# Cross-attention and expert layer: the queries split in two, the transposes one place sooner, the key split one place later

## What is computed

```
x = x + attention(layernorm(x), ctx)          # softmax(q k^T / 4) v, then @ Wp + bp
x = x + ffn(layernorm(x))                     # x <- the line above
# ffn: rms norm, logits = xn @ router^T + bias, probs = softmax(logits)
#      idx = top 512 rows per expert, y = gelu(xe @ fc1 + b1) @ fc2 + b2
#      the gated y are added into their rows and divided by the sum of the row's gates
```

## Time and profile before

| | |
|---|---|
| median of 3 runs | 991.97 us (991.0 to 992.49) |
| the profiled execution | 991.08 us, of which 989.3 us is the span of the instructions |
| TensorE busy over the span | 856.6 us (87%), weight loads 731.7 us (74%) |
| VectorE | 748.6 us (76%) |
| ScalarE | 507.9 us (51%) |
| GpSimd | 596.5 us (60%) |
| attention_phase | to about 475 us |

### The profile page before, as it was taken

One profiled execution on the slowest core, in us unless ns is written; L12 is line 12 of the kernel. 1 busy time (PEld: TensorE's weight loads), 2 busy tenths in 40 slices (PEclk: granted clock), 3 DMA queues, 4 the chain that ended last, 5 costly groups with the idle time before them and its releaser, 6 DMA issues. The chain is left out here.

```text
span 989.3 us, 20836 instructions
## 1 busy us (share of the span) xinstructions
PE 856.6 (87%) x6067; PEld 731.7 (74%) x6067; DVE 748.6 (76%) x1660; ACT 507.9 (51%) x921; POOL 596.5 (60%) x564
## 2 busy tenths in 40 slices
PE   3889999999999999999631138999999999999995
PEld 3677878878888878877521026989999999999985
DVE  4578888888888888887378975898777778777642
ACT  1355566555665566655246305555555555555531
POOL 3246676666766676656532265588887666775345
PEclk9799999999999999999855558999999999999998
DMA  4355666655665566654232024366766665665333
GB/s 146 101 196 200 199 207 220 215 200 188 221 220 203 200 201 218 222 191 152 80 109 85 4 65 136 115 169 171 208 169 161 157 159 154 159 163 158 94 70 43
DMA packets 129540, 156.51 MB, mean 158 GB/s; under 512 B 22464, under 2 KB 104656, under 8 KB 129376
## 3 DMA queue, kind: packets, MB, share of 16 engines
q1 hardware_dynamic: 104096, 113.06, 35.0%
q0 software_dynamic: 15616, 25.70, 12.3%
q10 hardware_dynamic: 9792, 17.31, 4.7%
HBM read 74.93 MB, written 26.28 MB: 102 GB/s over the span
## 5 line engine op out<-in xcount | busy, mean ns | idle before, releaser
L574 DVE TENSOR_REDUCE NM<-bank 128x4 f32<-128x480 f32 x256 | 155.7, 650 | 67.2 <-PE bank L724 66.4
L411 ACT ACTIVATE PT<-bank 120x512 f32<-120x512 f32 x256 | 144.3, 603 | 37.8 <-PE bank L749 35.4
L348 POOL TENSOR_SCALAR XN<-X,mv,rstd 128x256 f32<-128x256 f32 x126 | 153.1, 1225 | 14.4 <-POOL rstd L343 13.5
L1631 PE MATMUL bank<-W2H,HH 128*128 128x256 f32 x512 | 145.5, 284 | 2.0 <-issue 2.0
L1633 PE MATMUL bank<-W2H,HL 128*128 128x256 f32 x512 | 144.3, 282 | 0.0
L1632 PE MATMUL bank<-W2L,HH 128*128 128x256 f32 x512 | 144.2, 282 | 0.0
L1092 POOL DMA_INDIRECT out_dram<-C,IO x60 | 111.6, 1859 | 52.2 <-issue 31.0
L1360 DVE TENSOR_TENSOR HL<-hf,HH 128x512 fp32r<-128x512 f32 x128 | 87.3, 691 | 50.1 <-ACT HH L1515 49.4
L532 DVE RECIPROCAL RR<-RC 128x256 f32<-128x256 f32 x64 | 111.5, 1743 | 7.3 <-DMA RC<-PVS 7.3
L749 PE MATMUL bank<-QX,KX 128*120 128x256 f32 x512 | 110.0, 308 | 5.0 <-DMA QX<-NMT 4.6
L724 PE MATMUL bank<-KX,QX 128*128 128x240 f32 x512 | 105.4, 308 | 10.1 <-DMA QX<-QH 3.4
(11 more groups left out here) (189 smaller groups left out, 1894.1 us busy)
## 6 DMA issues: line engine op xcount, KB each, us to landing
QX<-QH ACTq DMA_DIRECT2D x64, 256.0 KB
W<-w1T_dram SPq DMA_DIRECT2D x16, 1024.0 KB, 5.4
W<-w2T_dram SPq DMA_DIRECT2D x16, 1024.0 KB, 5.9
X<-x_dram SPq DMA_DIRECT2D x32, 256.0 KB, 3.0
QX<-QL SPq DMA_DIRECT2D x32, 256.0 KB
XB<-x_dram SPq DMA_DIRECT2D x32, 256.0 KB, 2.9
RC<-PVS SPq DMA_DIRECT2D x64, 128.0 KB, 2.1
OC<-PVS SPq DMA_DIRECT2D x64, 128.0 KB, 3.0
```

Of the source, the lines that this page charges most:

```text
L348: ins = pool.tensor_scalar(dst[:, t, :], src[:, t, :], mv[:, t, 0:1], rstd[:, t:t + 1], ALU.subtract, ALU.mult)
L411: act.activation(PT[u][0:M, HE * k:HE * (k + 1), :], score_bank(b, k // 2)[k % 2][0:M, :], ACT.Exp, scale=SCALE) \
L574: dve.tensor_reduce(NM[u][:, t, :].rearrange("p (f n e) -> p n e f", n=HN, e=HE)[:, n, :, :], smax_bank[q % 2][:, 0:4 * M].rearrange("p (e ...
L1631: pe.matmul(o, wh, xh, start=first, stop=False)
```

## The change

Calls are put in another order on TensorE and VectorE; nothing is added or taken away, and ScalarE's, GpSimd's and SyncE's programs are the same. On VectorE `low_keys` goes behind the second row maximum. On TensorE the queries' product is made in two calls (its waits stand in the first, its signal q_done in the second), `queries(0)` before `max_scores(6)` and `queries(1)` before `max_scores(7)`; `rows2` goes before `scores(4)`, `rows` before `max_scores(2)` and `scores(5)`; and `scores(5)` goes behind `max_scores(2)`, `scores(6)` behind `max_scores(3)`, so that scores 6 and 7 stand side by side.

```diff
@@ VectorE, step
             row_sums(1)
+            row_max(0)
+            row_max(1)
             low_keys()
-            for q in range(4):
-                row_max(q)
+            row_max(2)
+            row_max(3)
             rows()
@@ TensorE, queries
-            def queries():
+            def queries(e):
...
-                    for e in range(HE):
-                        for k in range(KD):
-                            ins = pe.matmul(query_bank[:, e * S:(e + 1) * S], wq_sb[:, k, e * P:(e + 1) * P], XNT[u][:, k, :],
-                                            start=k == 0, stop=k == KD - 1)
-                    ins.then_inc(q_done, 1)
+                    for k in range(KD):
+                        ins = pe.matmul(query_bank[:, e * S:(e + 1) * S], wq_sb[:, k, e * P:(e + 1) * P], XNT[u][:, k, :],
+                                        start=k == 0, stop=k == KD - 1)
+                    if e == HE - 1:
+                        ins.then_inc(q_done, 1)
@@ TensorE, step
             max_scores(1)
+            rows2()
             scores(4)
-            rows2()
-            scores(5)
             rows()
             if last == 3:
                 turn_logits(1, 0, EARLY)
             max_scores(2)
+            scores(5)
+            max_scores(3)
             scores(6)
-            max_scores(3)
             scores(7)
             weigh(0)
             weigh(1)
             max_scores(4)
             max_scores(5)
-            queries()
+            queries(0)
             max_scores(6)
+            queries(1)
             max_scores(7)
```

More of the change, by code:

```diff
@@ L681, in rows @@
                     transpose_rows(xn_bank, XN[u], xnT_done)
-            def queries():
+            def queries(e):
                 b, u, j, live = batch(i, c, -2)
                 if live:
[L686 to L692, removed]
-                    for e in range(HE):
-                        for k in range(KD):
-                            ins = pe.matmul(query_bank[:, e * S:(e + 1) * S], wq_sb[:, k, e * P:(e + 1) * P], XNT[u][:, k, :],
-                                            start=k == 0, stop=k == KD - 1)
-                    ins.then_inc(q_done, 1)
+                    if e == 0:
+                        if known(b) and b == 0:
+                            pe.wait_ge(w_loaded, 16 * 7)
+                        pe.wait_ge(xnT_ready, b + 1)
+                        if known(b) and b < 5:
+                            wait(pe, ql_ready, b)
+                        else:
+                            pe.wait_ge(xn2T_ready, b - 4)
+                    for k in range(KD):
[3 more added lines that the diff above has]
+                        ins.then_inc(q_done, 1)
             def values():
```

## The result

Measured: 1000.87 us median (999.84 to 1002.97, 4 runs) against 991.49 (989.15 to 992.49, 4 runs). The ratio is 1.0117, with a 95% interval of 1.0092 to 1.0141: slower by 9 to 14 us. The two medians themselves lie 9.4 us apart, a quotient of 1.0095, at the low end of that interval. A later series gave 1.0112 (1.0085 to 1.0139), with medians of 1002.28 and 990.55. The forecast was 1004.2 us, 12.2 us slower.

A forecast was written before the change was run, and what follows sets the result against it. Bound: a loop of TensorE from max_scores(0) to weighing's end (8.15 us), then ScalarE and DMA (5.84). 0.49 less 0.04 is 0.45 us a step, 27 steps 12.2; on 991.08 plus 0.89 offset: 1004.2 us, range 997.5 to 1010.

The forecast's parts named there:

- The loop: Step of 13.99 us: TensorE from max_scores(0) to weighing's end, then ScalarE and QH's DMA; only these move the time.
- Part two: ScalarE's copies and QH DMAs, weighing's end to next max_scores(0), 5.84 us; table splits at the last weighing record's start.
- The wait of scores(7) for exp(5): TensorE, before weighing: scores(7) overwrites the bank exp(5) reads, so it waits 0.47 us where it never waited before.
- the low bound: Exp(5) starting 0.03 us behind its score instead of 0.11, with the DMA 0.13 quicker: 0.24 us a step, 6.5 us.
- The queries in halves: At maxima a 0.25 us gap closes; ScalarE gains 0.04 us, the other 0.21 goes into the wait at max_scores(0).
- The pair after a wait: Scores(7)'s matmul pair after its wait is 0.50 us long instead of 0.40, so weighing comes 0.10 later.
- the prediction's other case: At scores(7), weight loads pulled ahead would hide the 0.10 us, making the sum 2.7 us smaller.
- part one: TensorE from max_scores(0) to weighing's end, 8.15 us, forecast to grow 0.49; table splits at the last weighing record's start.
- its two steps: Steps 3 and 4, the ones before step 5 forecast to lose time, 0.45 us each.
- TensorE's gap is the bound: Rival: closing the gap at maxima shortens each step by 0.35 us, 27 steps 9.5 us, to 982.5 us; chance 0.06.
- The change doesn't do what it says: Rival: exp(5) is ready in time, the maxima gap only moves to max_scores(0), time stays 992 us; chance 0.07.
- SyncE's moves become the last: Rival: QL or RC lands late before max_scores(0), 0.3 us more a step, 8 us, to 1012 us; chance 0.08.

The follow-up runs named there:

- experiments 1 and 2: On the kernel before: first, only TensorE's new order from max_scores(1) to scores(7), ratio 1.0126; second, only the queries in halves around max_scores(6), ratio 0.9978.
- experiment 5: The full changed kernel, but with scores(7) moved behind weigh(0): 998.59 us, ratio 1.0090 to the kernel before.
- experiment 6: The kernel before, but ScalarE issues both QH DMAs right behind queries() instead of behind maxima(): 995.21 us, ratio 1.0059.

## Why the prediction was right, and where it was off

- **The loop.** Right. Part two is 6.13 to 6.20 us in nine rows of the table in which both QH DMAs are issued behind the maxima, whatever TensorE does, and 5.75 to 5.84 in the four with one early. (The 6.18 with both early is another path's, the one through the maxima.) The prediction's evidence was thinner than its claim: the 24 waits of weight loads are put down to "issue" and counted over all groups of L724, so they don't name the DMA. It is the semaphore's last update, 0.12 us before max_scores(0) in every steady step, that shows it.
- **The wait of scores(7) for exp(5).** Right in place and nearly in size: 0.39 us against 0.47, weighing at 3.63 against 3.72. The step that was mis-sized is "exp(5) starts 0.11 us behind the end of scores(5)": it started 0.03 behind (276.19 to 276.22), though ScalarE was idle. Exp(4), idle before it as well, took 0.12 (275.29 to 275.41). The 0.11 was read from exp(4), and I had 0.03 as the low bound, for a busy engine. But it doesn't go by idle or busy: exp(5) starts 0.03 to 0.05 behind its score in every steady step before and after, with ScalarE idle or not, and exp(4) 0.11 or 0.12 in 24 of 25. The trace of before had it in the other kind of step, where ScalarE was idle up to 0.07 us ahead of exp(5). The traces don't settle why the two differ.
- **The queries in halves.** The gap closed and went into the wait for QH, as forecast. It was 0.20 us and not 0.25: a group without a wait starts 0.07 ahead of the weighing's recorded end (282.12 against 282.19), and not 0.15. ScalarE gained 0.02 us in the mean, 0.04 was taken. Likewise pairs start 0.16 to 0.17 us ahead of the recorded end of the one before, not 0.12 (264.33 against 264.00 + 0.49); nothing in the sum hangs on that.
- **The pair after a wait.** 0.50 long at 276.87, as taken (0.50 in the mean of 25 steps, 0.40 before); the prediction's other case, a hidden weight load, would have had it 0.40.
- **Sum.** 0.40 to 0.42 us a step (0.45 forecast), and two misses offset each other in it: part one grew by 0.41 and not 0.49, and part two, from which 0.04 was taken off, stayed as it was (6.15 and 6.17 against 6.16). The 25 steady steps make 10.1 and 10.4 us in the two profiles of the changed kernel. Up to step 5 it lost 5.4 and 3.6 us where 0.9 was forecast, a term that the prediction put at nothing beyond its two steps. The rest of the program came out 3.5 and 0.2 us shorter, without a cause in the change. That makes the 11.9 and 13.7 us between the spans. The medians differ by 9.4 and 11.7 us; that they are so near to 12.2 is in part luck.
- **The rivals.** "TensorE's gap is the bound" fell with experiments 1 and 2. "The change doesn't do what it says" fell with the row at 276.87. "SyncE's moves become the last" came true in 1 of 25 steps of the changed kernel and in 11 of experiment 5, for 0.05 us a step.

## What to carry to other kernels

Before you close a gap on the busiest engine, follow the loop: ask which transfer ends the wait at the start of the next round and on whose queue it is issued; a gap in the part that waits for it anyway is worth nothing. When a producer is moved later past other work, count how much work is left between it and the consumer that reuses its buffer: here scores(5) and two more pairs (3 x 0.23 = 0.69 us) had to cover 1.08: a result (0.40), an exponential (0.60) and two hand-overs (0.03 and 0.05). The difference is the wait of 0.39. And try a cost in the company that it will have: the same order cost 0.41 us a steady step with one wait beside it and 0.11 with another.

## What the runs showed of the hardware

- Putting a score pair into the middle of the weighing (120 rows, 32 columns) costs 0.33 us (1.89 instead of 1.56, experiment 5), while the queries and two max_scores pairs take the same in one piece or in halves: 2.26 us before (268.82 to 271.08) and 2.27 now (278.85 to 281.12).
- A late move of the queries, 4.5 us instead of 2.7 to 3.0, left TensorE idle for 1.92 us, and its granted clock fell behind that, to a mean of 0.57 over 4 us.
- Two DMA issues stand on ScalarE's queue for 1.20 to 1.27 us; put into 0.8 us of idle time (experiment 6), they put the next copy off from 0.14 to 0.87 us behind its input in the mean.
- Exp(5) starts 0.03 to 0.05 us behind its score and exp(4) mostly 0.11 or 0.12, in the steady steps of all 14 profiles of the table. The cause is open.
